# Fourier attention and routed experts: the sum of v from the sum of x, kv evicted before a square, scatters in four pairs, one square moved to GpSimd

## The reference

```
q, k, v = x @ W.T + b, seen as 16 heads of 8
p       = (q or k) @ proj_mat / sqrt(8)             # 128 angles per head
feat    = [cos p, sin p] / sqrt(128)                # 256 features
kv      = sum over tokens of feat(k) x v            # 256 x 8 per head
out     = (feat(q) @ kv) @ Wo.T + bo
x1      = layernorm(x + out)
r       = softmax(x1 @ Wr + br), top 2 of 8 experts, rescaled to sum 1
y       = sum over the two experts of r_e * (relu(x1 @ W1_e + b1_e) @ W2_e + b2_e)
result  = layernorm(x1 + y)
```

## Time and profile before

| | |
|---|---|
| runs | 527.05, 527.19, 529.71 us; median 527.19 |
| the profiled execution | 527.94 us, span 526.1 us (1.84 us lie around the span) |
| PE busy | 484.8 us (92%) |
| DVE busy | 411.4 us (78%) |
| POOL busy | 393.2 us (75%) |
| ACT busy | 371.3 us (71%) |
| mean granted TensorE clock | 0.976 of full speed |

### The profile page before, as it was taken

One profiled execution on the slowest core, in us unless ns is written; L12 is line 12 of the kernel. 1 busy time (PEld: TensorE's weight loads), 2 busy tenths in 40 slices (PEclk: granted clock), 3 DMA queues, 4 the chain that ended last, 5 costly groups with the idle time before them and its releaser, 6 DMA issues.

```text
span 526.1 us, 12307 instructions
## 1 busy us (share of the span) xinstructions
PE 484.8 (92%) x3819; PEld 289.3 (55%) x3819; DVE 411.4 (78%) x897; ACT 371.3 (71%) x505; POOL 393.2 (75%) x463
## 2 busy tenths in 40 slices
PE   6699999999999999999999999878999999999813
PEld 3344344345345345345334444438999988999801
DVE  4878978979979888888888887567678976777554
ACT  3698797887898798788788786576555555565225
POOL 2374298888888889779779879985777787687645
PEclk9899999999999999999999999899999999999957
DMA  4563053144154143244233221032222333222184
GB/s 110 168 198 122 21 161 121 52 132 154 47 161 159 40 143 126 65 127 150 67 110 122 87 61 46 2 73 59 72 62 73 88 97 101 68 73 63 37 307 177
DMA packets 44596, 53.94 MB, mean 103 GB/s; under 512 B 8419, under 2 KB 25093, under 8 KB 44533
## 3 DMA queue, kind: packets, MB, share of 16 engines
q1 hardware_dynamic: 39728, 43.82, 28.1%
q0 software_dynamic: 4320, 8.95, 5.2%
q10 hardware_dynamic: 484, 0.38, 0.2%
HBM read 33.09 MB, written 20.04 MB: 101 GB/s over the span
## 4 chain that ended last, share of the span: by engine, by line
PE 67%; POOL 15%; DMA 4%; issue 4%; SPq 3%; DVE 3%; ACT 2%; DVEq 0%; POOLq 0%; ACTq 0%
PE misc L647 11%; PE ang L798 10%; PE ang L807 10%; PE ang L592 8%; PE misc L612 6%; PE ang L584 6%; POOL rows_s L1475 5%; PE ang L579 5%; POOL feats L1450 4%; PE misc L531 1%; POOL rstd L1468 1%; ACT feats L886 1%; PE misc L678 1%; PE misc L626 1%; PE misc L662 1%
## 5 line engine op out<-in xcount | busy, mean ns | idle before, releaser
L1073 DVE TENSOR_SCALAR turns<-ang 128x1024 f16<-128x1024 f32 x128 | 155.9, 1219 | 48.8 <-PE ang L584 29.7
L885 ACT ACTIVATE feats<-ang 128x1024 f32<-128x1024 f32 x128 | 131.3, 1026 | 63.1 <-PE ang L592 62.2
L1450 POOL TENSOR_TENSOR feats<-feats 128x1024 f32<-128x1024 f32 x56 | 107.8, 1925 | 58.8 <-ACT feats L886 58.4
L886 ACT ACTIVATE feats<-ang 128x1024 f32<-128x1024 f32 x128 | 131.1, 1024 | 0.0
L1081 DVE TENSOR_TENSOR feats<-feats 128x1024 f32<-128x1024 f32 x72 | 93.2, 1295 | 0.9 <-ACT feats L886 0.9
L1619 POOL DMA_INDIRECT routed_dram<-rows_s,slots x64 | 76.5, 1195 | 19.2 <-issue 18.2
L1649 POOL DMA_INDIRECT expert_dram<-feats x71 | 69.8, 983 | 25.8 <-DVE feats L1374 16.9
L592 PE MATMUL ang<-turns,negi 128*128 128x512 f16 x256 | 77.9, 386 | 4.0 <-DVE turns L1073 4.0
L798 PE MATMUL ang<-feats 128*128 128x128 f32 x568 | 76.5, 278 | 3.2 <-ACT feats L953 1.4
L953 ACT ACTIVATE feats<-experts 128x644 f32 x71 | 52.5, 739 | 34.9 <-DVE feats L1374 27.5
L807 PE MATMUL ang<-experts,feats 128*128 x568 | 75.6, 276 | 0.5 <-DVE feats L1334 0.5
(11 more groups left out here) (201 smaller groups left out, 570.1 us busy)
## 6 DMA issues: line engine op xcount, KB each, us to landing
stk<-parts_dram SPq DMA_DIRECT2D x126, 128.0 KB, 2.7
parts_dram<-parts SPq DMA_DIRECT2D x16, 512.0 KB, 3.3
feats<-routed_dram SPq DMA_DIRECT2D x72, 65.5 KB
experts<-ffn_W SPq DMA_DIRECT2D x16, 256.0 KB, 3.2
feats<-expert_dram SPq DMA_DIRECT2D x16, 256.0 KB, 4.8
out<-feats SPq DMA_DIRECT2D x8, 256.0 KB, 2.0
x_all<-attn_x SPq DMA_DIRECT2D x7, 256.0 KB, 4.5
expert_dram<-feats POOLq DMA_INDIRECT x71
```

The costliest lines, as they stand in the source:

```text
L885: act.activation(f[:, 0, :], a, ACT.Sin, scale=TWO_PI)
L886: act.activation(f[:, 1, :], a, ACT.Sin, scale=TWO_PI / 2).then_inc(s["sines"], 1)
L1073: dve.tensor_scalar(turns[:, u % 2, :], ang[:, slot(ph, u), :], MAGIC, -MAGIC, ALU.add, ALU.add)\
L1450: pool.tensor_tensor(f, f, f, ALU.mult).then_inc(s["sq_p"], 1)
```

## The change

The sum of v over the tokens isn't computed on PE by four products any more. VectorE's copy of the turned x also writes out the row sums (`x_sum`), one product of the v weights with that column gives the sum of v without its bias (`v_total`, step 9), and VectorE scales it and adds the bias part (`v_total_evac`, step 10). It goes into `kvT` at its copy, which is now in two parts: the half of the squares as 4 * value + sum, the other half plain. `kv_turn` becomes two transposes. The c product goes; VectorE sums `kvT` along its row instead (`c_evac`, step 14). The bias of v comes by four small DMAs on ScalarE's queue. On VectorE, `kv_evac`, `take_ranks` and `move_base` now stand right behind the rounding of step 12, and the square of unit 9 moves from step 11 to behind them. GpSimd squares unit 14 as well (in step 0 of the next sequence). The eight scatters of a sequence go out in four pairs: two in step 14, two in 15, two in step 0 of the next sequence, behind the square of unit 14, and two in step 1; those of sequence 6 end behind the square of unit 14 of sequence 7, all four at once.

```diff
--- before.py
+++ after.py
@@ -51,7 +51,7 @@
 N_WLOADS = 12
 N_SETUP = 4
 BO_STEPS = 10
-POOL_SQ = (1, 3, 4, 6, 8, 10, 12)
+POOL_SQ = (1, 3, 4, 6, 8, 10, 12, 14)
 TURN = 1.0 / (2.0 * math.pi * math.sqrt(DH))
 MAGIC = 12582912.0
 TWO_PI = 6.2831850051879883
@@ -115,9 +115,6 @@
         ident = sb("ident", [P, P])
         negi = sb("negi", [P, P], F16)
         mask = sb("mask", [P, G])
-        ident4 = sb("ident4", [P, P])
-        minus_2 = sb("minus_2", [P, P])
-        minus_half = sb("minus_half", [P, 2])
 
         w_raw = sb("w_raw", [P, 4, P])
         wo_perm = sb("wo_perm", [P, P])
@@ -179,8 +176,11 @@
         turns = sb("turns", [P, 2, UC], F16)
         feats = sb("feats", [P, HALF, 2, UC])
         kvT = sb("kvT", [P, 2, FEAT])
+        x_sum = sb("x_sum", [P, 2, 2])
+        bv_col = sb("bv_col", [P, 1])
+        v_sum = sb("v_sum", [P, 1])
+        c_raw = sb("c_raw", [P, 1])
         c_sum = sb("c_sum", [P, 1])
-        kv_c = sb("kv_c", [P, P])
         kv_pad = sb("kv_pad", [P, 2, G, HG * PADW])
         outT = sb("outT", [P, LEN])
         y = sb("y", [P, LT, P])
@@ -252,7 +252,7 @@
 
             "xT_mm", "xT_ev", "q_mm", "q_ev", "k_mm", "k_ev", "v_mm", "v_ev", "split", "parts_out",
 
-            "kvT_mm", "kvT_ev", "kv_mm", "kv_ev", "c_mm", "c_ev", "out_mm", "out_ev", "wo_mm",
+            "kvT_mm", "kvT_ev", "kv_mm", "kv_ev", "v_sum_mm", "v_sum_ok", "c_raw_ok", "c_ev", "bv_in", "bv_ok", "out_mm", "out_ev", "wo_mm",
 
             "y_ok", "bo_ok", "ln_stat", "ln_aggr", "ln_eps", "ln_pow", "ln_shift", "xn_ok", "xr_mm", "xr_ev",
 
@@ -616,22 +616,18 @@
                                        skip_group_check=True)
                 mm.then_inc(s["kvT_mm"], 1)
 
+            def v_total(b, *free):
+
+                wait(pe, *free)
+                pe.matmul(misc[:, 1, P:P + 2], wT[:, 2, :], x_sum[:, b % 2, :], start=True, stop=True,
+                          skip_group_check=True).then_inc(s["v_sum_mm"], 1)
+
             def kv_turn(b):
 
                 wait(pe, "kvT_ev", 1, b, 1)
-                o = misc[:, 0, :]
-                pe.matmul(o[:, 0:P], kvT[:, 0, :], ident[:, :], start=True, stop=True, skip_group_check=True)
-                pe.matmul(o[:, P:2 * P], kvT[:, 1, :], ident4[:, :], start=True, stop=False, skip_group_check=True)
-                for t in range(LT):
-                    mm = pe.matmul(o[:, P:2 * P], minus_2[:, :], dense(v_pad[:, t, :, :]),
-                                   start=False, stop=(t == LT - 1), skip_group_check=True)
+                for a in range(2):
+                    mm = pe.transpose(misc[:, 0, a * P:(a + 1) * P], kvT[:, a, :], ident[:, :])
                 mm.then_inc(s["kv_mm"], 1)
-
-            def c_product(b):
-
-                wait(pe, "kv_ev", 1, b, 1)
-                pe.matmul(misc[:, 0, 2 * P:2 * P + 2], kv_c[:, :], minus_half[:, :], start=True, stop=True)\
-                    .then_inc(s["c_mm"], 1)
 
             def out_product(b, hg, a, *free):
 
@@ -754,8 +750,10 @@
                         project(1, 1, b + 1, "k_ev", 1, b, 2)
                     if u == 8 and not first:
                         rows_T(b - 1, *(("b2_ok", 1, 0, 2) if last else ("q_ev", 1, b, 2)))
-                    if u == 9 and not first:
-                        logits(b - 1, "xr_ev", 1, b, 0)
+                    if u == 9:
+                        v_total(b, *(("q_ev", 1, b, 2) if first else ("xr_ev", 1, b, 0)))
+                        if not first:
+                            logits(b - 1, "xr_ev", 1, b, 0)
                     if u == 12:
                         kv_turn(b)
                         if not first:
@@ -764,12 +762,11 @@
                         out_product(b, 0, 0, *(("q_ev", 1, b, 2) if first else ("based", 1, b, 0)))
                         out_product(b, 0, 1)
                     if u == 14:
-                        c_product(b)
                         out_product(b, 1, 0)
                     if u == 15:
                         out_product(b, 1, 1)
                         if not last:
-                            v_product(b + 1, 0, "c_ev", 1, b, 1)
+                            v_product(b + 1, 0, "kv_ev", 1, b, 1)
 
 
             first_heads(0)
@@ -911,8 +908,11 @@
             for dst, src in ((bqk[0:1, :], bk.unsqueeze(0)), (bqk[1:2, :], bq.unsqueeze(0))):
                 act.dma_start(dst, src).then_inc(s["bias_in"], 16)
             act.dma_start(negi[:, :], c_negi).then_inc(s["negi_in"], 16)
+            for g in range(G):
+                act.dma_start(bv_col[g * PADH:(g + 1) * PADH, :],
+                              bv.rearrange("(a g d) -> g a d", a=HG, g=G)[g].unsqueeze(2)).then_inc(s["bv_in"], 16)
             act.dma_start(b1_raw[:, :], b1.rearrange("e (j p) -> (e j) p", p=P)).then_inc(s["b1_in"], 16)
-            act.wait_ge(s["consts"], 1)
+            act.wait_ge(s["consts"], 2)
             act.activation(warm[:, :], zero_t[:, :], ACT.Sin)
             act.wait_ge(s["raw_ev"], 1)
             proj_evac(0, 0, 1)
@@ -1001,15 +1001,17 @@
         @block.vector
         def _(dve):
             dve.memset(zero_t[:, :], 0.0).then_inc(s["consts"], 1)
-            dve.memset(minus_2[:, :], -2.0)
-            dve.memset(minus_half[:, :], -0.5)
+            dve.memset(x_sum[:, :, :], 0.0).then_inc(s["consts"], 1)
             dve.memset(eps_t[:, :], EPS)
             dve.memset(ones_b[:, :], 1.0)
             dve.memset(half_t[:, :], -0.5)
             dve.memset(part_32[:, :], 1.0 / 32)
             def x_evac(b):
                 wait(dve, "xT_mm", 1, b, 1)
-                dve.tensor_copy(xT[:, :], misc[:, 0, :]).then_inc(s["xT_ev"], 1)
+                if b == 0:
+                    dve.wait_ge(s["consts"], 2)
+                dve.tensor_scalar(xT[:, :], misc[:, 0, :], 1.0, 0.0, ALU.mult, ALU.add,
+                                  accum_out=x_sum[:, b % 2, 0:1]).then_inc(s["xT_ev"], 1)
 
             def permuted(w, bank, col):
 
@@ -1058,7 +1060,9 @@
             def late_setup():
 
                 dve.wait_ge(s["late_in"], 16 * 3)
-                dve.tensor_scalar(ident4[:, :], ident[:, :], 4.0, None, ALU.mult)
+                dve.wait_ge(s["bv_in"], 16 * G)
+                dve.tensor_scalar(bv_col[:, :], bv_col[:, :], -2.0 * LEN * KV_SCALE, None, ALU.mult)\
+                    .then_inc(s["bv_ok"], 1)
                 dve.tensor_copy(wo_perm[:, :].rearrange("p (g a d) -> p g a d", a=HG, g=G),
                                 w_raw[:, 3, :].rearrange("p (a g d) -> p g a d", a=HG, g=G)).then_inc(s["pad_ok"], 1)
                 for t in range(LT):
@@ -1080,25 +1084,33 @@
                 f = feats[:, u % HALF, 1, :]
                 dve.tensor_tensor(f, f, f, ALU.mult).then_inc(s["sq_v"], 1)
 
+            def v_total_evac(b):
+                wait(dve, "v_sum_mm", 1, b, 1)
+                dve.wait_ge(s["bv_ok"], 1)
+                dve.tensor_scalar(v_sum[:, :], misc[:, 1, P:P + 1], -2.0 * KV_SCALE, bv_col[:, :],
+                                  ALU.mult, ALU.add).then_inc(s["v_sum_ok"], 1)
+
             def kvT_evac(b):
                 wait(dve, "kvT_mm", HALF, b, HALF)
-                dve.tensor_copy(kvT[:, :, :].rearrange("p a m -> p (a m)"), misc[:, 0, 0:2 * P])\
-                    .then_inc(s["kvT_ev"], 1)
+                wait(dve, "v_sum_ok", 1, b, 1)
+                dve.tensor_scalar(kvT[:, 1, :], misc[:, 0, FEAT:2 * FEAT], 4.0, v_sum[:, :], ALU.mult, ALU.add)
+                dve.tensor_copy(kvT[:, 0, :], misc[:, 0, 0:FEAT]).then_inc(s["kvT_ev"], 1)
 
             def kv_evac(b):
                 wait(dve, "kv_mm", 1, b, 1)
 
                 wait(dve, "out_mm", HG, b, 0)
-                dve.tensor_copy(kv_c[:, :], misc[:, 0, P:2 * P])
                 dve.tensor_copy(dense(kv_pad[:, :, :, :].rearrange("p a g w -> p (a g) w")),
                                 misc[:, 0, 0:2 * P].rearrange("p (g a d) -> p g a d", a=HG, d=DH))\
                     .then_inc(s["kv_ev"], 1)
 
             def c_evac(b):
-                wait(dve, "c_mm", 1, b, 1)
+                wait(dve, "kvT_ev", 1, b, 1)
+                dve.tensor_reduce(c_raw[:, :], kvT[:, 1, :], AX.X, ALU.add).then_inc(s["c_raw_ok"], 1)
+                wait(dve, "c_raw_ok", 1, b, 1)
 
                 wait(dve, "out_ev", 1, b, 0)
-                dve.tensor_copy(c_sum[:, :], misc[:, 0, 2 * P:2 * P + 1]).then_inc(s["c_ev"], 1)
+                dve.tensor_scalar(c_sum[:, :], c_raw[:, :], -0.5, None, ALU.mult).then_inc(s["c_ev"], 1)
 
             def v_evac(b, bank):
                 wait(dve, "v_mm", 1, b, 1)
@@ -1267,9 +1279,9 @@
 
             LAST_ROUND = ((7, bias_add), (8, bias_add))
 
-            BEFORE_ROUND = ((6, moments), (10, take_logits), (13, move_base))
-            AFTER_ROUND = ((5, residual), (10, largest))
-            AFTER_SQUARE = ((5, statistics), (10, which), (12, take_ranks), (13, slot_numbers))
+            BEFORE_ROUND = ((6, moments), (10, take_logits))
```

(19 more changed lines are left out.)

## The result

| | before | after |
|---|---|---|
| median of the runs | 528.12 us (4 runs, 527.05 to 529.71) | 537.64 us (4 runs, 536.90 to 538.49) |
| the profiled execution | 527.94 us, span 526.1 | 538.34 us, span 536.5 |
| PE busy | 484.8 us | 481.3 us |
| DVE, POOL busy | 411.4, 393.2 us | 427.9, 410.1 us |

What follows compares the result with a forecast made beforehand. PE was taken as the bound, busy 40.73 of 41.0 us in a middle sequence. Losses of 7 x 1.30 = 9.1 plus 1.0 in the last sequence took 527.94 to 538.0; less 0.75 for the median, 537.3 us, range 520 to 540.

Steps and rivals of the forecast that it cites:

- TensorE's products: PE, per sequence: removed or cheaper products save 0.89 + 0.22 + 0.12 us, v_total adds 0.24; 0.99 less.
- the wait for the base: PE in step 12: 0.1 us of the 0.99 saved per sequence stays lost waiting for the base.
- VectorE's small edits: Split kvT copy, v-sum step, c reduction and accumulating x copy on VectorE: lie in slack or idle time, cost nothing.
- The pick sum: GpSimd's L1600: takes 0.25 us instead of 1.09 once square 9 no longer runs beside it.
- Square 9: VectorE, step 12: held by GpSimd's square 10, ends at 169.38; PE's second output product loses 0.6 us.
- The race: Steps 12 to 13: GpSimd's square 12 beats VectorE's square 11 by 0.14 us; reduction 14 loses 1.45, a sequence 1.30.
- the order is kept: Rival: VectorE comes to square 11 first; seven sequences make -2.1 us, the last +1.0: 526.1, no change; chance 0.19.
- the round held 0.14 us later in the sequence: VectorE's late round around 185.3: GpSimd's sums still delay rounds by about the old 0.14 us, so no gain.
- The last sequence, 1.0: Sequence 7: square 14 behind four scatters ends between 351.8 and 353.0; PE's last output product loses 0.3 to 1.5, taken 1.0.
- the saving comes through: Rival: squares don't meet as said, 0.93 us gained per sequence, 6.5 over seven, less 1.0: 521.7; chance 0.28.
- GpSimd outright the bound: Rival: late square 1 or 3 stalls key-value products; up to 0.5 us per sequence on six: 540.5; chance 0.05.

Runs made afterwards that it cites:

- swap_nine: Changed kernel with squares 9 and 10 exchanged between GpSimd and VectorE, square 14 back on VectorE, scatters four and four: 519.90 us, ratio 0.985.
- order: Changed kernel with one wait added: GpSimd's square 12 waits for VectorE's square 11; 533.77 us, ratio 1.013.
- swap: Changed kernel with squares 9 and 10 exchanged: GpSimd squares 9 and 12, VectorE 10 and 11 behind round 13; 529.41 us, ratio 1.004.
- nine: Changed kernel with square 14 back on VectorE, all else kept, scatters in four pairs: 534.46 us, ratio 1.011.
- order_nine: Changed kernel with GpSimd's square 12 waiting for VectorE's square 11, square 14 on VectorE, scatters four and four: 524.05 us, ratio 0.993.
- last: Changed kernel, but in the last sequence GpSimd's square 14 goes behind two scatters instead of four: 534.01 us, ratio 1.013.
- four_four: Changed kernel with all eight scatters in steps 14 and 15 as before, square 14 on GpSimd behind them: 567.64 us, one run.

## Why the prediction was right

537.3 us were forecast, 537.64 measured. The mechanism was the one named; part of the agreement in the sum is luck. Step by step, times of after with 1.84 taken off:

- **TensorE's products.** Forecast 0.99 less, with 0.24 for v_total. In the trace v_total is 0.25, kv_turn 0.22 (168.04 to 168.26). In swap_nine, where nothing else waits, the sequence fell by 0.72 only: the first output product stands 0.71 behind its reduction, where 0.56 was, and two reductions 0.07 and 0.04 later behind their angles. The first of these is the wait for the base, put at 0.1 among the rivals.
- **VectorE's small edits at nothing.** They lie under other work: kvT in two parts 0.35 and 0.28, v_sum 0.20, c_raw 0.27, the accumulating copy 0.68 as before plus a read of 0.08. The Trainium skill (VectorE: DVE Perf Modes, "Two Vector instructions with no wait between them") counts an accumulator output as a second instruction; the trace agrees, with that row of 0.08 us.
- **The pick sum** at 0.25: it is.
- **Square 9** to end at 169.38: it ended at 169.37. The first output product came at 167.95 as forecast and the second, due at 168.88, at 169.42: 0.54 lost for the 0.6 forecast. The profile's 0.40 is the idle time alone.
- **The race.** Forecast: GpSimd at 170.28, VectorE at 170.42; measured 170.25 and 170.42. Square 11 to end at 173.26, it did at 173.23; reduction 14 at 174.59, it was 174.54. From start to start the loss is the 1.45 forecast, of which 1.28 show as idle time. In sequence 0 the forecast margin was 0.09, the measured one 0.08. That this race makes the middle's loss is shown by taking it away: its gap is gone in order and swap, where another collision takes its place; from nine to order_nine the sequence falls by 1.44, to 40.82, and there it is 0.18 shorter than before, where the rival "the order is kept" had 0.16. That the eighth square isn't the cause is shown by nine.
- **"No gain" from the round held 0.14 us later in the sequence.** Here the step failed: that late reduction is gone (0.58 behind its angles, 0.71 before). The v product came 1.25 later in the sequence, and the whole grew by 1.11, not 1.30. The gain comes from square 14 on GpSimd, since nine and swap_nine, with nine squares on VectorE, have the late reduction still. Over seven: 8.0 for 9.1.
- **The last sequence, 1.0.** Mis-sized. Square 14 ended at 352.75 in the clock of before (6.42 off), inside the 351.8 to 353.0 forecast. But TensorE wanted it at 350.5, a microsecond ahead of the 351.56 assumed. That number held two waits for the experts' rows in the kernel before, of which TensorE met only one of 0.59 now:

```profile
349.24 0.33 PE L787 MATMUL ang<-ident,feats 128*128 128x128 f32 x1 [0.65 <-DMA feats<-routed_dram]
350.37 0.33 PE L787 MATMUL ang<-ident,feats 128*128 128x128 f32 x1 [0.80 <-DMA feats<-routed_dram]
```

  And no term stood for the clock: after the gap it ran low for some 5 us. In all 2.27 up to the experts and 1.20 behind, with 0.54 in the last pass; last and nine, which are without the gap, gave back 3.6 and 3.2. The part behind the first expert group is the least sure: in the eight traces that have neither the late square 14 nor the low stretch behind it, it takes from 172.4 to 174.2 us, in the changed kernel 175.3.
- **The start** was 1.60 shorter and no term stood for it. The low clock of the first 30 us lay over the start's waits in after (0.78 in 14 to 20 us) and over key-value products in before (0.81 in 24 to 30). The other traces show that the execution makes this, and not the change: order runs the same instructions as after up to step 14 of sequence 0, and had the low clock late as before had it (0.84 in 24 to 30 us) and the same group at 29.78, where after had it at 28.31.

The errors are -1.1, -1.6 and +3.0 us and nearly cancel, and the second of them is the chance of one execution. The rival "the saving comes through" at 521.7 exists, as swap_nine, with another assignment of squares. GpSimd outright the bound didn't occur; its price in the prediction, 0.5 on six sequences, makes 540.3 and not the 540.5 written there. four_four, which puts all eight scatters ahead of square 14, shows a mechanism of that kind at ten times the price (30 us, one run).

## What to carry to other kernels

Where two engines exclude each other for whole instructions, write down who arrives first at each meeting and by how much, before moving anything: here 0.17 us of 40 decided over 1.45 us per sequence. The starts of the rows are a guide to that, not proof: in four_four the engine whose row started first by 0.46 was the one that waited. Taking work off the bounding engine pays only when the engine that feeds it is not delayed on the way; test the saving and the reordering each alone and together, since neither shortened a middle sequence by more than 0.02 by itself, and both together took 0.72 off. A repair of one collision is to be checked against the next one down the queue: it moves one engine and not the other, and in order and in swap that brought two later squares together.

## What the runs showed that was not expected

- A VectorE square can wait out two GpSimd squares in a row: 5.30 us (four_four). Its end is 1.10 us after the second (195.24 + 3.74 = 198.98, 194.78 + 5.30 = 200.08).
- When VectorE's squares come first and GpSimd's square waits, the wait is shorter and hits nobody: 2.72 for 1.89 (swap_nine), against 2.81 for 1.21 on VectorE in the changed kernel.
- Scatters wait for VectorE's squares too. In the twelve traces with a result, from 80 to 320 us, 246 scatters were issued while a VectorE square had at least 0.13 us to go, and every one ended 0.81 to 0.89 us after that square, taking 0.97 to 1.97 us; the other 322 took 0.95 to 1.23. So how long four scatters take depends on where the squares stand beside them, and a price of one scatter holds only for its place.
- A gap of 2.37 us on TensorE (2.71 in order and swap) was followed by some 5 us at a granted clock near the lower level (0.55 here), and so by a group of 2.08 us for 1.16; the gap cost more than itself.
- A small DMA of one value per partition (bv_col) holds ScalarE's queue for 0.70 us, not the 0.45 assumed from its others; it lay in the idle time at the start.
